# Second cross attention: the relative scores of a unit read back from DRAM as one transfer of 1 MB, behind the slot's store

## The chip, the cores and the metric

The kernel runs as one program on one core of one Trainium2 chip. The metric is the device time in microseconds (us), the median of three runs. Profile times count from the start of the profiled execution's span.

## What is computed

The reference is a small two-layer Perceiver: 256 latent tokens of width 256 attend to a context of 4096 rows, then go through self attention and a mixture of experts, twice. All of it is float32. The change lies in the cross attention of the second layer, which is a relative-position attention with 16 heads of 16 columns:

```python
content = jnp.einsum('bthd,bThd->bhtT', q + r_w_bias, k)
pe = _sinusoid_reversed(b, kv_t, DMODEL) @ Wp + bp
rel = jnp.einsum('bthd,bThd->bhtT', q + r_r_bias, pe)
rel = _relative_shift(rel)          # pad one column, read with another pitch
attn = (content + rel) * (1.0 / math.sqrt(HEAD_DIM))
attn = attn * mask - 10000000000.0 * (1.0 - mask)
p = jax.nn.softmax(attn, axis=-1)
out = jnp.einsum('bhtT,bThd->bthd', p, v)
```

The shift turns the 256 x 4096 scores of a head into rows that begin at another place: each row of 4096 scores gets a zero in front, so that rows lie 4097 apart, and the result is the same memory read with a pitch of 4096 from element 256 on.

## The kernel before, in words

`cross1` works in 64 units: 16 heads, 2 tiles of 128 queries, 2 halves of 2048 keys (16 x 2 x 2). Four units (U = 4) belong to a head. A unit of 128 x 2048 scores is handled in two parts of 128 x 1024 (SUB); here they are called its left half (part 0) and its right half (part 1).

The relative scores make a round trip through DRAM, which does the shift. For unit n + 4 TensorE computes them in slot n (`relative`, L1761), ScalarE copies both halves from PSUM into `out0` or `out1` (`evacuate`, L1886), and SP stores the unit, 1 MB, into the tensor `rel_scores` with a pitch of 4097 (`store`, L1711). Two slots later, SP reads the unit back with a pitch of 4096 into `row`, which holds eight units (`read_back`, L1698). A unit read back needs the stores of its own head that its shifted rows touch, up to the store of the unit after it.

In unit n's own slot VectorE adds the content scores from PSUM to the row (`add`, L1968), half by half; GpSimd multiplies each half with the mask (L1938, one instruction a half); VectorE takes the maximum of each half of the unit before (`top_of`, L1979); ScalarE applies the exponential to the whole unit before (`exponentials`, L1891). Three slots behind, TensorE transposes the row (`turn`, L1805), ScalarE copies the transposes (L1897), and TensorE weighs the values with them (`weigh`, L1818).

Each engine runs a hand-written list of steps per slot, with semaphores between engines. `slots` runs the filling slots -4 to 3, then a hardware loop of six passes over eight slots, then the last slots. An engine does its steps strictly in order:

- VectorE in slot n: left add of n, left maximum of n-1, right add of n, right maximum of n-1.
- ScalarE: left transposes' copy of n-3, left copy of n+4, right transposes' copy of n-3, exponential of n-1, right copy of n+4.
- TensorE: right relative scores of n+3, left content scores of n, left transposes of n-3, left relative scores of n+4, right content scores of n, right transposes of n-3, weighted sums of n-3. Content scores share one PSUM buffer, so the right ones wait for the left add.
- SP: the keys of a head to come (512 KB, once in four slots) or its values (272 KB, once in four), then left half-read of n+2, store of n+4, right half-read of n+2. The left read waits for the stores that it needs; the store waits for ScalarE's right copy.

VectorE's add of a half waits for that half's own semaphore, `rel_back[u][part]`, and for the content scores in PSUM. All transfers here are issued on SP's queue.

Of the kernel before, what the change touches and what calls it, by code (L numbers as in the profile page):

```python
# [21 lines left out]
P = 128  # L22
# [1564 lines left out]
U = NT * NHALF  # L1587
SUB = HALF // 2
CPS = SUB // P
UNITS = H * U  # L1590
ROWS_HELD = 2 * U
# [3 lines left out]
def cross1(f, mask, qw):  # L1595
# [8 lines left out]
    with ExitStack() as ctx:  # L1604
# [7 lines left out]
        with ExitStack() as inner:  # L1612
# [8 lines left out]
            rel_back = [[f.sem(f"b_rel_back{n}_{part}") for part in range(2)] for n in range(U)]  # L1621
# [65 lines left out]
            def _(sp):  # L1687
                def read_back(p, c, part, first=False):
                    n, head, u, b, t, half = where(p, c)
                    if not first:  # L1690
                        sp.wait_ge(s["turned"], 2 * n + part + 1)
                        sp.sem_inc(s["row_free"], 1)

                    for k in ((0, 1), (0, 1, 2), (2, 3), (2, 3))[u] if part == 0 else ():
                        sp.wait_ge(rel_stored[k], 16 * (head + 1))
                    columns = slice(part * SUB, (part + 1) * SUB)
                    src = rel_back_view[half][bass.ds(head, 1), t * P:(t + 1) * P, columns]
                    sp.dma_start(row[:, held(c):held(c) + 1, columns], src.rearrange("h p n -> p h n")  # L1698
                                 ).then_inc(rel_back[u][part], 16)
# [17 lines left out]
                def slot(p, c, n):  # L1717
# [11 lines left out]
                    begins = n is not None and n == -2  # L1729
                    if runs(n, 2):  # L1730
                        read_back(p, c + 2, 0, first=n is not None and n + 2 < ROWS_HELD)
                    if runs(n, 2) and begins:
                        read_back(p, c + 2, 1, first=True)
                    if runs(n, U):
                        store(p, c + U)
                    if runs(n, 2) and not begins:
                        read_back(p, c + 2, 1, first=n is not None and n + 2 < ROWS_HELD)
# [207 lines left out]
            def _(dve):  # L1945
# [16 lines left out]
                def add(p, c, part):  # L1962

                    n, head, u, b, t, half = where(p, c)
                    dve.wait_ge(rel_back[u][part], 16 * (head + 1))
                    dve.wait_ge(s["cont_mm"], 2 * n + part + 1)
                    at = part * SUB
                    nc.vector.tensor_tensor(row[:, held(c), at:at + SUB], cont_ps[:], row[:, held(c), at:at + SUB],  # L1968
                                            ALU.add).then_inc(s["cont_out"], 1)
# [772 lines left out]
```

## Time and profile before

| | |
|---|---|
| median of three runs | 1371.69 us (1367.45 to 1372.56) |
| profiled execution | 1370.89 us, its span 1369.1 us |
| mean granted TensorE clock in it | 0.929 |
| TensorE, ScalarE, VectorE, GpSimd busy | 82%, 65%, 60%, 46% of the span |
| second cross attention | about 720 to 1211 us |
| DMA traffic of the whole span | 257.53 MB, mean 188 GB/s |
| reads back in the span | 128 of 512 KB, median 6.6 us from issue to landing |
| stores of relative scores | 64 of 1 MB, median 6.1 to 6.2 us |

### The profile page before, as it was taken

To read this page: it belongs to the slowest core of one execution; us is meant where nothing else is said; L and a number is where in the kernel's file an instruction comes from. 1 tells how busy PE (TensorE), PEld (TensorE's weight loads), DVE (VectorE), ACT (ScalarE), POOL (GpSimd) and SP (SyncE) were. 2 spreads that over 40 slices of the span, in tenths; PEclk is the share of its full clock that TensorE was granted. 3 is DMA by queue.
4 is the path that set the end of the run, shared out by engine and by line. 5 is a ranking of instruction groups with operands and counts; after the bars stand their busy time and mean duration, and the time that the engine had idled before them with its cause. 6 is when DMAs were issued, how large, how long until landed. Compare 5 with 4: busy or idle time off the path is not lost. (4 is left out here: it accounts for less than half of the span.)

```text
span 1369.1 us, 25496 instructions
## 1 busy us (share of the span) xinstructions
PE 1122.3 (82%) x8423; PEld 686.5 (50%) x8423; DVE 822.0 (60%) x1502; ACT 893.6 (65%) x1204; POOL 632.2 (46%) x297
## 2 busy tenths in 40 slices
PE   7677887748999859989977878888888888858798
PEld 3343443423444346678862445455454544434687
DVE  5688888861111176562235778888888887835312
ACT  3599999967999624533323788888888888624110
POOL 2277887850000005000003889999999999900000
PEclk9899999978999968999985899999999999967899
DMA  7875455447554071024467989999999998533130
GB/s 247 256 225 134 118 130 136 116 97 158 106 113 93 0 229 45 1 70 151 152 229 255 322 292 327 327 325 332 308 324 325 327 329 311 179 114 127 47 138 8
DMA packets 97051, 257.53 MB, mean 188 GB/s; under 512 B 11193, under 2 KB 41305, under 8 KB 85466
## 3 DMA queue, kind: packets, MB, share of 16 engines
q1 hardware_dynamic: 96992, 256.79, 59.6%
q8 instruction: 32, 0.52, 0.2%
q14 instruction: 27, 0.22, 0.1%
HBM read 165.31 MB, written 91.92 MB: 188 GB/s over the span
## 5 line engine op out<-in xcount | busy, mean ns | idle before, releaser
L1938 POOL TENSOR_TENSOR xb_row<-xb_row,w_mask 128x1024 f32<-128x1024 f32 x128 | 419.1, 3286 | 237.4 <-DVE xb_row L1968 235.8
L1968 DVE TENSOR_TENSOR xb_row<-xb_cont_ps,xb_row 128x1024 f32<-128x1024 f32 x128 | 156.7, 1224 | 84.6 <-PE xb_cont_ps L1761 67.9
L1761 PE MATMUL xb_rel_ps<-xb_kk,xb_qq 32*128 32x512 f32 x496 | 150.0, 683 | 34.8 <-ACT xb_out L1886 33.2
L553 DVE TENSOR_REDUCE xa_stats<-xa_b_ps 128x1 f32<-128x1024 f32 x128 | 155.8, 1219 | 27.2 <-PE xa_b_ps L469 25.9
L1979 DVE CUSTOM_DVE_ANT_0 xb_row<-xb_row,xb_minus 128x1024 f32<-128x1024 f32 x128 | 170.4, 1331 | 0.0
L1891 ACT ACTIVATE xb_row<-xb_row,xb_ntop 128x2048 f32<-128x2048 f32 x64 | 128.3, 2005 | 53.8 <-DVE xb_ntop L1985 53.8
L1761 PE MATMUL xb_cont_ps<-xb_kk,xb_qq 32*128 32x512 f32 x528 | 160.2, 684 | 1.5 <-DVE xb_qq L2040 1.1
L868 ACT ACTIVATE xa_probs<-xa_psT,xa_t_now 128x1024 f32<-128x1024 f32 x128 | 141.2, 1114 | 24.6 <-PE xa_psT L825 24.5
L1886 ACT COPY xb_out<-xb_rel_ps 128x1024 f32<-128x1024 f32 x124 | 124.7, 1005 | 39.5 <-PE xb_rel_ps L1761 26.2
L521 ACT ACTIVATE xa_exps<-xa_b_ps,xa_stats 128x1024 f32<-128x1024 f32 x128 | 140.7, 1101 | 4.2 <-DVE xa_stats L553 4.2
L1897 ACT COPY xb_turned<-xb_turn_ps 128x1024 f32<-128x1024 f32 x126 | 127.5, 1012 | 23.2 <-PE xb_turn_ps L1805 21.1
L1805 PEld LDWEIGHTS xb_turn_ps<-_ident,xb_row 128*128 128x128 f32 x1008 | 114.7, 147 | 55.8 <-issue 55.8
L1805 PE MATMUL xb_turn_ps<-_ident,xb_row 128*128 128x128 f32 x1008 | 137.2, 280 | 5.9 <-ACT xb_turned L1897 5.1
L639 POOL TENSOR_TENSOR xa_rest<-xa_exps 128x1024 f32<-128x1024 f32 x48 | 90.9, 1894 | 90.8 <-ACT xa_exps L521 85.5
L1818 PE MATMUL xb_sum_ps<-xb_turned,xb_vhead 128*17 128x128 f32 x2048 | 81.3, 276 | 37.5 <-ACT xb_turned L1897 36.5
L1408 POOL TENSOR_TENSOR b_tc<-b_raw,w_waves 128x512 f32<-128x512 f32 x4 | 5.1, 1270 | 222.3 <-ACT b_raw L1394 222.3
L469 PE MATMUL xa_b_ps<-xa_k,xa_q 96*128 96x512 bf16 x256 | 69.8, 384 | 24.3 <-ACT xa_exps L521 13.9
L531 ACT ACTIVATE xa_squares<-xa_exps 128x1024 f32<-128x1024 f32 x80 | 84.4, 1055 | 3.0
L798 PE MATMUL xa_sums<-xa_probs,xa_vhead 128*17 128x256 f32 x1024 | 81.3, 390 | 0.2 <-ACT xa_probs L868 0.2
L490 PE MATMUL xa_b_ps<-xa_wv,xa_ctxT 128*128 x512 | 67.0, 285 | 16.0 <-ACT xa_exps L521 16.0
L1818 PEld LDWEIGHTS xb_sum_ps<-xb_turned,xb_vhead 128*17 128x17 f32 x2048 | 45.0, 97 | 66.8 <-ACT xb_turned L1897 54.7
L490 PEld LDWEIGHTS xa_b_ps<-xa_wv,xa_ctxT 128*128 128x128 f32 x512 | 61.1, 195 | 31.5 <-ACT xa_exps L521 26.4
(367 smaller groups left out, 1821.9 us busy)
## 6 DMA issues: line engine op xcount, KB each, us to landing
xb_row<-rel_scores SPq DMA_DIRECT2D x128, 512.0 KB, 6.6
rel_scores<-xb_out SPq DMA_DIRECT2D x32, 1024.5 KB, 6.2
rel_scores<-xb_out SPq DMA_DIRECT2D x32, 1024.0 KB, 6.1
b_e_w<-in_L_ffn_e_w SPq DMA_DIRECT2D x32, 513.0 KB, 3.5
w_w<-in_L_ffn_w SPq DMA_DIRECT2D x24, 512.0 KB, 4.5
xa_k<-first_parts SPq DMA_DIRECT2D x24, 384.0 KB, 4.9
value_rows<-xa_values SPq DMA_DIRECT2D x16, 544.0 KB, 6.1
xb_kk<-key_blocks SPq DMA_DIRECT2D x17, 512.0 KB, 8.2
```

The costliest lines, as they stand in the source:

```text
L490: mm = nc.tensor.matmul(out[:, n * P:(n + 1) * P], ctxT[:, k, at:at + P], wv[:, bass.ds(it, 1), k, :], start=(k == 0), stop=(k == KC - 1))
L521: nc.scalar.activation(exps[:, u % 4], ps[:, slot % 4], ACT.Exp, scale=-1.0, bias=stats[:, c % 2, 0, u:u + 1], accum_out=stats[:, c % 2, 1 ...
L553: nc.vector.tensor_reduce(stats[:, c % 2, 0, u:u + 1], ps[:, slot % 4], AX, ALU.min).then_inc(s["min_ready"], 1)
L868: nc.scalar.activation(probs[:, g % 4].rearrange("p c n -> p (c n)"), ps[:, g % 2], ACT.Exp, scale=t_now[:, b:b + 1]).then_inc(probs_ready, 1)
L1761: mm = nc.tensor.matmul(out[:, k * BANK:(k + 1) * BANK], qq[rows, b, kind, t * P:(t + 1) * P], kk[rows, b, half], start=True, stop=True)
L1805: mm = nc.tensor.transpose(out_ps[:, k * P:(k + 1) * P], row[:, held(c), at:at + P], f.ident[:])
L1818: mm = nc.tensor.matmul(sum_ps[at:at + DV, 0:P], vhead[:, b, half * NCH // 2 + part * CPS + k, :], turned[:, part, k, :], start=(part == 0 ...
L1891: nc.scalar.activation(row[:, held(c)], row[:, held(c)], ACT.Exp, bias=ntop[:, u:u + 1]).then_inc(s["exp_done"], 1)
L1897: nc.scalar.copy(turned[:, part].rearrange("p k n -> p (k n)"), turn_ps[:]).then_inc(turned_sb[part], 1)
L1938: nc.gpsimd.tensor_tensor(row[:, held(c), at:at + SUB], row[:, held(c), at:at + SUB], mask[:, t, half * HALF + at:half * HALF + at + SUB], ...
L1968: nc.vector.tensor_tensor(row[:, held(c), at:at + SUB], cont_ps[:], row[:, held(c), at:at + SUB], ALU.add).then_inc(s["cont_out"], 1)
L1979: nc.vector.tensor_tensor_reduce(out=row[:, held(c), at:at + SUB], in0=row[:, held(c), at:at + SUB], in1=minus[:, t, half * HALF + at:half ...
```

## The change

`read_back` loses its argument `part`. One transfer of 128 x 2048 float32 (1 MB, rows of 8 KB instead of 4 KB) replaces the two of 128 x 1024. It has one semaphore for each of the four units of a head, so both adds of a unit wait for the same landing. In the filling slots -2 and -1 it is issued ahead of the slot's store; in all others behind it, where until now only the right half's read stood. It waits for both transposes of the unit that held its row buffer before. The order of the steps on the other engines stays.

```diff
--- before.py
+++ after.py
@@ -1618,7 +1618,7 @@
             k_loaded, v_loaded = ([f.sem(f"{n}_loaded{b}") for b in range(2)] for n in ("k", "v"))
             turned_sb = [f.sem(f"b_turned_sb{n}") for n in range(2)]
             rel_stored = [f.sem(f"b_rel_stored{n}") for n in range(U)]
-            rel_back = [[f.sem(f"b_rel_back{n}_{part}") for part in range(2)] for n in range(U)]
+            rel_back = [f.sem(f"b_rel_back{n}") for n in range(U)]
             kk = f.sb(inner, "kk", [P, 2, NHALF, BANK])
             vhead = f.sb(inner, "vhead", [P, 2, NCH, DV])
             wq = f.sb(inner, "wq", [P, KC, D + HEAD_PAIR])
@@ -1685,18 +1685,16 @@
 
             @block.sync
             def _(sp):
-                def read_back(p, c, part, first=False):
+                def read_back(p, c, first=False):
                     n, head, u, b, t, half = where(p, c)
                     if not first:
-                        sp.wait_ge(s["turned"], 2 * n + part + 1)
+                        sp.wait_ge(s["turned"], 2 * n + 2)
                         sp.sem_inc(s["row_free"], 1)
 
-                    for k in ((0, 1), (0, 1, 2), (2, 3), (2, 3))[u] if part == 0 else ():
+                    for k in ((0, 1), (0, 1, 2), (2, 3), (2, 3))[u]:
                         sp.wait_ge(rel_stored[k], 16 * (head + 1))
-                    columns = slice(part * SUB, (part + 1) * SUB)
-                    src = rel_back_view[half][bass.ds(head, 1), t * P:(t + 1) * P, columns]
-                    sp.dma_start(row[:, held(c):held(c) + 1, columns], src.rearrange("h p n -> p h n")
-                                 ).then_inc(rel_back[u][part], 16)
+                    src = rel_back_view[half][bass.ds(head, 1), t * P:(t + 1) * P]
+                    sp.dma_start(row[:, held(c):held(c) + 1], src.rearrange("h p n -> p h n")).then_inc(rel_back[u], 16)
 
                 def store(p, c):
                     n, head, u, b, t, half = where(p, c)
@@ -1726,15 +1724,13 @@
                         if n is None or n > U:
                             sp.wait_ge(s["weighed"], 2 * U * (2 * p + c // U) + 2)
                         load_values(p, c + U)
-                    begins = n is not None and n == -2
-                    if runs(n, 2):
-                        read_back(p, c + 2, 0, first=n is not None and n + 2 < ROWS_HELD)
-                    if runs(n, 2) and begins:
-                        read_back(p, c + 2, 1, first=True)
+                    filling = n is not None and n < 0
+                    if runs(n, 2) and filling:
+                        read_back(p, c + 2, first=True)
                     if runs(n, U):
                         store(p, c + U)
-                    if runs(n, 2) and not begins:
-                        read_back(p, c + 2, 1, first=n is not None and n + 2 < ROWS_HELD)
+                    if runs(n, 2) and not filling:
+                        read_back(p, c + 2, first=n is not None and n + 2 < ROWS_HELD)
 
                 def load_values(p, c):
                     b = c // U % 2
@@ -1962,7 +1958,7 @@
                 def add(p, c, part):
 
                     n, head, u, b, t, half = where(p, c)
-                    dve.wait_ge(rel_back[u][part], 16 * (head + 1))
+                    dve.wait_ge(rel_back[u], 16 * (head + 1))
                     dve.wait_ge(s["cont_mm"], 2 * n + part + 1)
                     at = part * SUB
                     nc.vector.tensor_tensor(row[:, held(c), at:at + SUB], cont_ps[:], row[:, held(c), at:at + SUB],
```

## Rows read from the trace of the kernel before

**Rows 1.** The page's costliest groups: busy us, mean ns of one, idle before.

```profile
L1938 POOL TENSOR_TENSOR xb_row<-xb_row,w_mask 128x1024 f32<-128x1024 f32 x128 | 419.1, 3286 | 237.4 <-DVE xb_row L1968 235.8
```

**Rows 2.** SP's register moves by instruction, tile rel_scores, whole span.

```profile
L1711 SPq MOVE rel_scores<-xb_out x48: 29/29/35, 776.1 to 1112.1; - x48
```

**Rows 3.** 900:1000: length; busy PE, PEld, DVE, ACT, POOL; PEclk, DMA share, GB/s.

```profile
900.00:1000.00 100.00, 83.45 (x939) 48.93 (x938) 81.18 (x147) 83.53 (x75) 92.17 (x29) 1.00 0.92 318
```

**Rows 4.** Waits, 760 to 1180: us in total, times, longest.

```profile
POOL xb_row L1938 <- DVE xb_row L1968: 33.8, 66, 1.1
...
DVE xb_row L1968 <- DMA xb_row<-rel_scores: 15.9, 18, 1.6
```

**Rows 5.** VectorE in order of time: start us, us, instruction, idle before.

```profile
903.82 1.22 DVE L1968 TENSOR_TENSOR xb_row<-xb_cont_ps,xb_row 128x1024 f32<-128x1024 f32 x1 [0.61 <-PE xb_cont_ps L1761]
...
907.12 1.23 DVE L1968 TENSOR_TENSOR xb_row<-xb_cont_ps,xb_row 128x1024 f32<-128x1024 f32 x1 [0.85 <-PE xb_cont_ps L1761]
908.26 1.23 DVE L1979 CUSTOM_DVE_ANT_0 xb_row<-xb_row,xb_minus 128x1024 f32<-128x1024 f32 x1
...
918.08 1.23 DVE L1968 TENSOR_TENSOR xb_row<-xb_cont_ps,xb_row 128x1024 f32<-128x1024 f32 x1 [0.72 <-PE xb_cont_ps L1761]
...
921.25 1.23 DVE L1968 TENSOR_TENSOR xb_row<-xb_cont_ps,xb_row 128x1024 f32<-128x1024 f32 x1 [0.72 <-PE xb_cont_ps L1761]
```

**Rows 6.** ScalarE in order of time.

```profile
909.78 2.01 ACT L1891 ACTIVATE xb_row<-xb_row,xb_ntop 128x2048 f32<-128x2048 f32 x1 [0.61 <-DVE xb_ntop L1985]
911.69 0.99 ACT L1886 COPY xb_out<-xb_rel_ps 128x1024 f32<-128x1024 f32 x1
```

**Rows 7.** SP's queue in order of time.

```profile
906.00 0.35 SPq L1711 DMA_DIRECT2D rel_scores<-xb_out  x1
...
911.85 0.33 SPq L1698 DMA_DIRECT2D xb_row<-rel_scores  x1
912.84 0.35 SPq L1711 DMA_DIRECT2D rel_scores<-xb_out  x1
913.53 0.33 SPq L1698 DMA_DIRECT2D xb_row<-rel_scores  x1
```

**Rows 8.** Right-half reads issued at 906.70, 913.53, 920.74, 927.90: KB, us to landing.

```profile
xb_row<-rel_scores SPq DMA_DIRECT2D x1, 512.0 KB, 7.1
...
xb_row<-rel_scores SPq DMA_DIRECT2D x1, 512.0 KB, 7.5
...
xb_row<-rel_scores SPq DMA_DIRECT2D x1, 512.0 KB, 7.2
...
xb_row<-rel_scores SPq DMA_DIRECT2D x1, 512.0 KB, 6.4
```

**Rows 9.** Left-half read issued at 911.85; store issued at 722.49, nothing else in flight.

```profile
xb_row<-rel_scores SPq DMA_DIRECT2D x1, 512.0 KB, 4.9
...
rel_scores<-xb_out SPq DMA_DIRECT2D x1, 1024.5 KB, 4.2
```

**Rows 10.** TensorE in order of time.

```profile
905.90 0.70 PE L1761 MATMUL xb_cont_ps<-xb_kk,xb_qq 32*128 32x512 f32 x2
...
906.43 0.59 PE L1761 MATMUL xb_cont_ps<-xb_kk,xb_qq 32*128 32x512 f32 x2
```

**Rows 11.** Three stretches: length, PEclk, DMA share, GB/s.

```profile
724.00:726.70 2.70, 0.50 0.68 276
...
909.00:911.00 2.00, 1.00 0.95 252
1180.00:1185.00 5.00, 1.00 0.80 315
```

**Rows 12.** Content matmuls of 738 to 758, then of 900 to 1000: mean ns.

```profile
L1761 PE MATMUL xb_cont_ps<-xb_kk,xb_qq 32*128 32x512 f32 x24 | 12.5, 1136 | 0.0
...
L1761 PE MATMUL xb_cont_ps<-xb_kk,xb_qq 32*128 32x512 f32 x112 | 31.6, 639 | 0.0
```

**Rows 13.** TensorE, 1190 to 1195: length, busy, PEclk, DMA share, GB/s.

```profile
1190.00:1195.00 5.00, 3.10 (x49) 1.00 0.02 3
```

## The prediction

> **What bounds the kernel now.** I read the page's costliest groups first, then the stretches, the waits, and last single slots in order of time. The change touches only the second cross attention, some 490 us of the span; the chain of work that ended last lies in the final stage and says nothing of it. There GpSimd's mask multiplication is the largest single load: 3.29 us a half, 6.57 us a unit [rows 1]. The stores inside the hardware loop, each with one register move, show a unit's period: 48 of them from 776.1 to 1112.1 us, so 336.0/47 = 7.15 us [rows 2]. In 900 to 1000 us GpSimd is busy 92%, the DMA engines 92%, TensorE 83%, ScalarE 84% and VectorE 81% [rows 3]. Nothing is saturated, but four engines and the DMA stand close together, and GpSimd's gaps are waits for VectorE's add (33.8 us in all), while adds waited for a read from DRAM 18 times, 15.9 us together [rows 4]. So the slot is a ring of dependences, and the question is which ring a later landing closes.
>
> **The ring that the reads close.** Take the slot whose first add starts at 903.82 and call its unit m. The add of its right half starts at 907.12 [rows 5]; the right-half maximum of m-1 follows it, ScalarE's exponential starts at 909.78, the copy of the right half of m+4 at 911.69 [rows 6], and SP issues the store of m+4 at 912.84 and the right-half read of m+2 at 913.53 [rows 7]. That read takes 7.5 us [rows 8] and lands at 921.03; the right add of m+2 starts at 921.25 [rows 5]. So this ring spans two slots, and it has 0.2 us of slack: the right half arrives only just in time. The left half is another matter: issued at 911.85 [rows 7], 4.9 us long [rows 9], it lands at 916.75, and its add starts at 918.08 [rows 5], 5.24 us after the store was issued.
>
> **What the change removes and adds.** Per unit one issue of 512 KB ahead of the store goes, and the read behind the store grows from 512 KB to 1 MB. The bytes are the same. What is new is that the left add waits for the end of the whole transfer.
>
> SP's saved issue costs about 0.33 us of SP time [rows 7], and SP waits for ScalarE's copy anyway (it ends at 912.68, the store is issued at 912.84): nothing, and if that cover were gone 0.7 us a slot of earlier store at most. The wait for a free row buffer now asks for both transposes instead of one; they belong to the unit eight before, five slots back: nothing. The waits for the stores of other units move behind the store of m+4, by when they have mostly been met (the one issued at 906.00 let the left read go at 911.85): nothing. In the two filling slots before unit 0 both halves are read ahead of the store; one 0.5 MB read moves there, once: under 2 us.
>
> The term that counts is the ring. After the change the left add of m+2 waits for the landing, and from it the ring runs:
> - left add to right add. Today 907.12 - 903.82 = 3.30 us, but TensorE's content matmuls there waited for ScalarE's copy of the slot before, which with a longer slot ends in time. What remains is the add's 1.14 us (908.26 - 907.12, by the next start), some 0.1 us to TensorE, the matmuls from 905.90 to 906.43 + 0.59 = 907.02, and the 0.1 us from there to the add [rows 5, 10]: 1.14 + 0.1 + 1.12 + 0.1 = 2.46 us.
> - right add to store: 912.84 - 907.12 = 5.72 us, all of it serial (add, maximum, exponential, copy) [rows 5 to 7].
> - store to landing. The four slots of a head give 7.1, 7.5, 7.2 and 6.4 us for the right half [rows 8], and it is issued 0.70 us behind the store [rows 7]: 7.05 + 0.70 = 7.75 us on average. All four drain the same 2 MB (left half, store, right half), though the left half had up to 1.5 us of lead, or in one slot in four had mostly gone. After the change nothing of these 2 MB leads, but the queue ahead is emptier. I keep 7.75.
> - landing to add: 0.1 us.
>
> The sum is 2.46 + 5.72 + 7.75 + 0.10 = 16.03 us for two slots, 8.02 us a slot, 0.87 more than 7.15. Reads behind a store are those of units 2 to 61, 60 of them: 60 x 0.87 = 52 us. The profiled execution took 1370.9 us (span 1369.1, 1.8 around it), close to the median of 1371.7; 1370.9 + 52 = **1423 us**, 3.8% slower. GpSimd, TensorE and ScalarE get 0.9 us of idle time a slot and start nothing sooner for it; behind the waiting left add VectorE's two maxima of m-1 stand in its queue, behind the second one the exponential and the copy that lets the store go, and TensorE's right content matmul with the transposes and weighted sums behind it.
>
> **Bounds.** Store to landing is the unknown. From below: a store with nothing else in flight took 4.2 us [rows 9], and a second MB at the rate of a stretch of reads alone, 315 GB/s at a share of 0.80, so 394 at a full one [rows 11], adds 2.66: 6.9 us, 15.18 for two slots, 7.59 a slot, +26 us, 1397. From above: the longest of the four, 0.70 + 7.5 = 8.2 us, with the left-to-right step not shortened (3.30): 17.3 us for two slots, 8.66, +91 us, 1462. 7.75 lies near the rows of the same bytes in the same traffic, and those decide. The Trainium skill ("DMA: Bandwidth & Descriptors", Anatomy of one DMA) fits a transfer as 2.0 us fixed plus its bytes at 436 GB/s, fitted on another issuing path; for the 2.1 MB of store and read that is an estimate of 6.8 us and a total near 1394. The trace stands above it here: 512 KB would be 3.2 us, and 4.9 were measured in traffic [rows 9].
>
> **Rivals.**
> *The merged read makes the stage faster* (4%). For it: the DMA engines are at 0.92 and pay for changes of direction: in 909 to 911 us, where a store gives way to a read, they moved 252 GB/s at a share of 0.95 [rows 11], against 394, so some 0.7 us lost. Left, store, right has two such changes a unit, store and whole read one less. Longer packets give 276/0.68 = 406 against 394 GB/s [rows 11], 3%, 0.08 us a unit. If the DMA's load set the pace, the slot would fall until GpSimd's 6.57 and a gap of 0.2 stop it: 6.8 us, -0.35 x 60 = -21 us, 1350. It decides only if 2.1 MB land within the 5.24 us in which the left add is due. Against it: the right half, behind fewer bytes, needed 7.1 us at least. The Trainium skill ("DMA: Bandwidth & Descriptors", Bandwidth) advises transfers of at least 1 MiB for three quarters of the peak rate, which speaks for this rival; rows of transfers of 1 MB and 512 KB here differ by those 3%.
> *No change that can be measured* (6%): the ring has slack. It needs a landing within 14.30 - 2.46 - 5.72 - 0.10 = 6.0 us of the store; 1371. Only much faster draining of an emptier queue would give that.
> *TensorE's clock falls* (5%). Its busy share drops to 0.83 x 7.15/8.02 = 0.74, with a wait of over 1 us in every slot. Score matmuls average 639 ns at the full clock and 1136 at the half one [rows 12]; 0.83 x 7.15 = 5.9 us of work a slot would become 5.9 x 1136/639 = 10.5 and set the slot: with a tenth of the slots so, 6 x 2.5 = 15 us more than the forecast, 1438; with all, +200 over now, 1571. Against it: at the end of the stage a stretch with TensorE busy 62% was still granted 1.00 [rows 13]. The Trainium skill ("TensorE: Matmul & The Clock Gate", HAM oscillation) says that a wait for a transfer in each round of a loop can bring the half clock back every time.
>
> **How the numbers follow.** The ring has 85% and its own range, 1397 to 1462. Of the rest, 4% lies at 1350, 6% at 1371 and 5% above 1438. A range of 1395 to 1460 leaves out the first two (10%), the far half of the clock case (3%) and some 5% at the ring's edges. Faster by over 0.5% (6.9 us, about what a measurement of this kernel can tell from no change) 4%, within it 6%, slower 90%.
>
> **What would show it.** The period of the stores in the loop at 8.0 us (7.15); adds waiting for the read nearly 60 times, each 1 to 2 us, all on left halves; the right add about 2.5 us behind the left one; the store issued some 8.2 us after the left add (9.0); store to landing 7.75 us; GpSimd busy 82% in the stage, the DMA share about 0.82; 60 to 64 issues of 1 MB. The prediction is wrong if the merged read lands within 6 us of the store, or if the half-clock shows in the stage.

## The result, and the profile after

The changed kernel takes **1447.35 us** (median of 4, 1443.79 to 1450.38), against 1370.14 for the kernel before in the same comparison: **1.0567 times as long, interval 1.054 to 1.0595**. The forecast was 1423 us, with a range of 1395 to 1460. The direction and the range held; the forecast is 24 us too low. The profiled execution took 1447.24 us, its span 1445.4, 76.3 more than before.

The period of a slot, by SP's register moves in the loop (answers to [rows 2]), and who waited for the transfers of this tile in the whole span:

```profile
L1709 SPq MOVE rel_scores<-xb_out x48: 29/29/35, 781.7 to 1173.3; - x48
...
who waited for it (us, times):
  DVE xb_row L1964: 103.9, 55
```

(1173.3 - 781.7)/47 = 8.33 us a slot. It was 7.15; I forecast 8.02. The 47 intervals of the loop make 47 x 1.18 = 55.5 us of the 76.3. From the first store of all to the last, 63 intervals, the stores now take 72.6 us more, so 17 us come in the slots outside the loop; of the last 3.7, 3.4 lie behind the last store and 0.3 ahead of the first.

The stretch 900 to 1000 us (answers to [rows 3]: busy PE, PEld, DVE, ACT, POOL; granted clock, DMA share, GB/s), and the waits from 780 to 1240 us, in total, times, longest (answers to [rows 4]):

```profile
900.00:1000.00 100.00, 82.86 (x802) 46.67 (x804) 76.55 (x126) 70.59 (x63) 78.95 (x24) 0.95 0.76 274
```

```profile
POOL xb_row L1934 <- DVE xb_row L1964: 98.8, 57, 3.9
DVE xb_row L1964 <- DMA xb_row<-rel_scores: 90.4, 49, 3.6
ACT xb_row L1887 <- DVE xb_ntop L1981: 66.7, 52, 1.5
```

GpSimd fell from 92% to 79%, the DMA engines from 0.92 to 0.76. All engines got idle time, and the adds wait for the read 49 times instead of 18, 90.4 us instead of 15.9: a ring of waits sets the pace, no engine's load. TensorE's own share hides half-clock work, taken up below.

The ring itself, first VectorE in order of time (answers to [rows 5]; start, length, idle before):

```profile
916.47 1.22 DVE L1964 TENSOR_TENSOR xb_row<-xb_cont_ps,xb_row 128x1024 f32<-128x1024 f32 x1 [2.54 <-DMA xb_row<-rel_scores]
917.61 1.22 DVE L1975 CUSTOM_DVE_ANT_0 xb_row<-xb_row,xb_minus 128x1024 f32<-128x1024 f32 x1
...
918.92 1.23 DVE L1964 TENSOR_TENSOR xb_row<-xb_cont_ps,xb_row 128x1024 f32<-128x1024 f32 x1
920.06 2.07 DVE L1975 CUSTOM_DVE_ANT_0 xb_row<-xb_row,xb_minus 128x1024 f32<-128x1024 f32 x1
922.06 0.08 DVE L1975 DVE_READ_ACCUMULATOR2_ANT xb_top<- 128x1 f32 x1
...
924.30 1.23 DVE L1964 TENSOR_TENSOR xb_row<-xb_cont_ps,xb_row 128x1024 f32<-128x1024 f32 x1 [0.56 <-DMA xb_row<-rel_scores]
```

Then ScalarE's exponential and right copy (answers to [rows 6]), and SP's queue (answers to [rows 7]):

```profile
922.42 2.00 ACT L1887 ACTIVATE xb_row<-xb_row,xb_ntop 128x2048 f32<-128x2048 f32 x1 [1.41 <-DVE xb_ntop L1981]
924.33 0.99 ACT L1882 COPY xb_out<-xb_rel_ps 128x1024 f32<-128x1024 f32 x1
```

```profile
908.79 0.35 SPq L1709 DMA_DIRECT2D rel_scores<-xb_out  x1
909.54 0.33 SPq L1697 DMA_DIRECT2D xb_row<-rel_scores  x1
...
916.70 0.36 SPq L1709 DMA_DIRECT2D rel_scores<-xb_out  x1
917.57 0.34 SPq L1697 DMA_DIRECT2D xb_row<-rel_scores  x1
925.49 0.35 SPq L1709 DMA_DIRECT2D rel_scores<-xb_out  x1
```

And the time to landing of the store issued at 908.79 and of the read issued at 909.54, KB and us, from the DMA view (answers to [rows 8, 9]):

```profile
rel_scores<-xb_out SPq DMA_DIRECT2D x1, 1024.0 KB, 4.9
...
xb_row<-rel_scores SPq DMA_DIRECT2D x1, 1024.0 KB, 6.8
```

The read of 909.54 lands at 916.34, and the left add that needs it starts at 916.47. From there: left add to right add 918.92 - 916.47 = 2.45 us; right add to store 925.49 - 918.92 = 6.57; store to landing 916.34 - 908.79 = 7.55; landing to add 0.13. That is 16.70 us for two slots, 8.35 a slot; the loop's mean is 8.33. Left add to store is 9.02 to 9.04 us in 45 of the 48 loop slots; the other three come up below.

| term | forecast | measured |
|---|---|---|
| left add to right add | 2.46 | 2.45 |
| right add to store | 5.72 | **6.57** |
| store to landing | 7.75 | 7.55 (7.1 to 8.8 in the loop's slots, 7.45 as their mean) |
| landing to add | 0.10 | 0.13 |
| a slot | 8.02 | 8.35 |

**Where the 0.85 us come from.** The page's groups of the two instructions that stand beside each other in time, busy us and mean ns of one (the first answers to [rows 1]):

```profile
L1934 POOL TENSOR_TENSOR xb_row<-xb_row,w_mask 128x1024 f32<-128x1024 f32 x128 | 419.0, 3291 | 315.7 <-DVE xb_row L1964 315.5
...
L1975 DVE CUSTOM_DVE_ANT_0 xb_row<-xb_row,xb_minus 128x1024 f32<-128x1024 f32 x128 | 201.3, 1573 | 0.0
```

The same maxima averaged 1331 ns in the kernel before:

```profile
L1979 DVE CUSTOM_DVE_ANT_0 xb_row<-xb_row,xb_minus 128x1024 f32<-128x1024 f32 x128 | 170.4, 1331 | 0.0
```

Their work is unchanged, yet the right maximum at 920.06 is 2.07 us long where the left one is 1.22. GpSimd's row of the same moment, two mask instructions in a row:

```profile
917.77 6.58 POOL L1934 TENSOR_TENSOR xb_row<-xb_row,w_mask 128x1024 f32<-128x1024 f32 x2 [2.21 <-DVE xb_row L1964]
```

The left mask ends at 917.77 + 3.29 = 921.06, and the right maximum at about 922.13, 1.07 us behind it. The kernel before has the same distance. Its GpSimd in order of time, then its VectorE:

```profile
905.12 6.59 POOL L1938 TENSOR_TENSOR xb_row<-xb_row,w_mask 128x1024 f32<-128x1024 f32 x2 [0.26 <-DVE xb_row L1968]
...
919.38 6.59 POOL L1938 TENSOR_TENSOR xb_row<-xb_row,w_mask 128x1024 f32<-128x1024 f32 x2 [0.47 <-DVE xb_row L1968]
```

```profile
922.40 1.34 DVE L1979 CUSTOM_DVE_ANT_0 xb_row<-xb_row,xb_minus 128x1024 f32<-128x1024 f32 x1
```

Left masks end there at 908.41 and 922.67, right maxima at 908.26 + 1.23 = 909.49 [rows 5] and 922.40 + 1.34 = 923.74: 1.08 and 1.07 us later. Of the mask's typical 3283 ns its shortest record, with no maximum beside it, needs 2343; so it stretches too. By these records a maximum and a mask instruction don't run side by side: whichever starts second waits, and the wait is inside its record, not in front of it. It is so throughout: of the 44 slots 8 to 51, 42 have a right maximum longer than 1.3 us in this kernel and 22 in the kernel before, and every one of them ends 1.08 to 1.09 us after the left mask (unrounded times; 1.07 by the rounded rows above). An add (one operand in PSUM) is 1.22 to 1.23 us long beside a mask in both kernels. So the way from left add to store is left add 1.14, left maximum 1.14, the left mask's own 2.34, and 1.07 of right maximum, about 5.7 us, and then exponential and copy. The right add lies beside it. It comes 3.30 us after the left one in the kernel before and 2.45 in this one, and the store still goes 9.02 us after the left add in both (912.84 - 903.82 [rows 5, 7]; 925.49 - 916.47).

The Trainium skill ("GPSIMD Engine Reference", Specifications) has GpSimd sharing its SBUF interfaces with VectorE and contending with VectorE's instructions that have two SBUF inputs; the maximum is one (scores and mask term), the add is not. The trace agrees; the size, about 1 us for each of the two, is the runs'.

### The profile page after: what moved, and what is told of

The parts are those of the page before. It is cut to its first block and busy times, and to the rows that moved or that the text cites. A ratio compares the mean times of both kernels' runs of the same rounds, so it can differ in the third digit from the quotient of the medians.

```text
span 1445.4 us, 25230 instructions
## 1 busy us (share of the span) xinstructions
PE 1180.1 (82%) x8423; PEld 709.4 (49%) x8423; DVE 852.8 (59%) x1502; ACT 893.0 (62%) x1204; POOL 632.2 (44%) x297
## 5 line engine op out<-in xcount | busy, mean ns | idle before, releaser
L1975 DVE CUSTOM_DVE_ANT_0 xb_row<-xb_row,xb_minus 128x1024 f32<-128x1024 f32 x128 | 201.3, 1573 | 0.0
L1757 PE MATMUL xb_cont_ps<-xb_kk,xb_qq 32*128 32x512 f32 x528 | 166.2, 708 | 11.3 <-DVE xb_row L1964 9.8
L1893 ACT COPY xb_turned<-xb_turn_ps 128x1024 f32<-128x1024 f32 x126 | 127.5, 1012 | 73.1 <-PE xb_turn_ps L1801 72.6
L1801 PEld LDWEIGHTS xb_turn_ps<-_ident,xb_row 128*128 128x128 f32 x1008 | 121.4, 153 | 55.3 <-issue 55.3
L1801 PE MATMUL xb_turn_ps<-_ident,xb_row 128*128 128x128 f32 x1008 | 146.4, 292 | 2.2 <-ACT xb_turned L1893 1.8
L1814 PE MATMUL xb_sum_ps<-xb_turned,xb_vhead 128*17 128x128 f32 x2048 | 89.9, 299 | 33.0 <-ACT xb_turned L1893 30.9
L1814 PEld LDWEIGHTS xb_sum_ps<-xb_turned,xb_vhead 128*17 128x17 f32 x2048 | 48.2, 103 | 67.8 <-ACT xb_turned L1893 52.2
L1757 PEld LDWEIGHTS xb_rel_ps<-xb_kk,xb_qq 32*128 32x128 f32 x496 | 40.2, 198 | 81.2 <-ACT xb_out L1882 64.6
```

Source lines behind the costliest of these rows:

```text
L1757: mm = nc.tensor.matmul(out[:, k * BANK:(k + 1) * BANK], qq[rows, b, kind, t * P:(t + 1) * P], kk[rows, b, half], start=True, stop=True)
L1801: mm = nc.tensor.transpose(out_ps[:, k * P:(k + 1) * P], row[:, held(c), at:at + P], f.ident[:])
L1814: mm = nc.tensor.matmul(sum_ps[at:at + DV, 0:P], vhead[:, b, half * NCH // 2 + part * CPS + k, :], turned[:, part, k, :], start=(part == 0 ...
L1893: nc.scalar.copy(turned[:, part].rearrange("p k n -> p (k n)"), turn_ps[:]).then_inc(turned_sb[part], 1)
L1975: nc.vector.tensor_tensor_reduce(out=row[:, held(c), at:at + SUB], in0=row[:, held(c), at:at + SUB], in1=minus[:, t, half * HALF + at:half ...
```

## The experiments

The comparisons are with the kernel before on the same chip (medians 1369.5 to 1371.5). A period is that of SP's register moves in the loop, as above. Line numbers differ from kernel to kernel.

**The place of the read.** Three kernels separate where the read stands from how large it is. The first keeps the one transfer of 1 MB but issues it ahead of the store in every slot.

```diff
-                    filling = n is not None and n < 0
-                    if runs(n, 2) and filling:
-                        read_back(p, c + 2, first=True)
+                    if runs(n, 2):
+                        read_back(p, c + 2, first=n is not None and n + 2 < ROWS_HELD)
                     if runs(n, U):
                         store(p, c + U)
-                    if runs(n, 2) and not filling:
-                        read_back(p, c + 2, first=n is not None and n + 2 < ROWS_HELD)
```

> The changed kernel with the 1 MB read issued ahead of the slot's store everywhere instead of behind it. Theory (position: what costs is that the left half's landing moved behind the store, and a ring of two slots closes through it): the read goes when the store of the slot before lands, the ring becomes one of three slots, 9.0 us from left add to store, some 6.5 from store to landing, some 6 for the read, so 21.6/3 = 7.2 us a slot, near the kernel before: 1370 to 1390 us. Rival (size: a transfer of 1 MB as such comes too late wherever it stands): a slot of 8.3 us as in the changed kernel, about 1447.

Measured: 1427.69 us, ratio 1.0415 (1.0366 to 1.0465), period 8.04. Neither theory gave this. One turn, on VectorE, then SP's queue, then the landing of the store of 902.20 and of the read of 910.81:

```profile
891.51 1.22 DVE L1961 TENSOR_TENSOR xb_row<-xb_cont_ps,xb_row 128x1024 f32<-128x1024 f32 x1 [0.28 <-PE xb_cont_ps L1754]
...
917.38 1.23 DVE L1961 TENSOR_TENSOR xb_row<-xb_cont_ps,xb_row 128x1024 f32<-128x1024 f32 x1 [1.97 <-DMA xb_row<-rel_scores]
```

```profile
901.58 0.33 SPq L1697 DMA_DIRECT2D xb_row<-rel_scores  x1
902.20 0.35 SPq L1709 DMA_DIRECT2D rel_scores<-xb_out  x1
...
910.81 0.34 SPq L1697 DMA_DIRECT2D xb_row<-rel_scores  x1
```

```profile
rel_scores<-xb_out SPq DMA_DIRECT2D x1, 1024.0 KB, 8.4
...
xb_row<-rel_scores SPq DMA_DIRECT2D x1, 1024.0 KB, 6.4
```

The store behind 1 MB of read lands after 8.4 us, not 4.9, and the next read that needs its rows is issued 0.2 us after it has landed (902.20 + 8.4 = 910.6). So another ring closes, over three slots. This turn of it is 917.38 - 891.51 = 25.9 us: left add to store 10.7, store 8.4, 0.2, read 6.4, and the rest to the add; 8.6 us a slot. The mean period is less, because the read of a head's fourth unit needs no store of the slot before it and goes early. Left add to store is no longer fixed: it goes from 9.0 to 12.6 us in the loop, once to 14.0, since ScalarE waits 31 times, 60.0 us in the span, for the landing of a store that gives back an out buffer (the adds wait 70.3 us, 33 times, for a read). Which of the two waits is worth how much stays open. The merged read is slower than the kernel before in either place.

The second keeps two halves, and issues both behind the store (the filling slots as in the changed kernel).

```diff
-                    if runs(n, 2):
-                        read_back(p, c + 2, 0, first=n is not None and n + 2 < ROWS_HELD)
...
                     if runs(n, U):
                         store(p, c + U)
-                    if runs(n, 2) and not begins:
-                        read_back(p, c + 2, 1, first=n is not None and n + 2 < ROWS_HELD)
+                    if runs(n, 2) and not filling:
+                        for part in range(2):
+                            read_back(p, c + 2, part, first=n is not None and n + 2 < ROWS_HELD)
```

> Only the position of the change, not its size: two reads of 512 KB, both behind the store, each add with its own semaphore. Theory (each add waits for its own bytes, so part of the loss is the merging and part the position): the left half lands some 1.3 to 1.5 us before the whole did, 6.0 us after the store instead of 7.4, and the ring gives (9.0 + 6.0 + 0.1)/2 = 7.55 us a slot, about 1400 us. Rival (position alone costs all): 8.3 us a slot, about 1447. Rival (merging alone costs all): 7.15 us, about 1371.

Measured: 1427.56 us, 1.0423 (1.0365 to 1.0481), period 8.02. It lies between the theory's 1400 and the rival's 1447: the left half lands 6.9 us after the store, not 6.0. VectorE in order of time, for the left half issued at 910.71 behind the store of 909.85:

```profile
900.81 1.22 DVE L1968 TENSOR_TENSOR xb_row<-xb_cont_ps,xb_row 128x1024 f32<-128x1024 f32 x1 [1.68 <-DMA xb_row<-rel_scores]
...
916.87 1.23 DVE L1968 TENSOR_TENSOR xb_row<-xb_cont_ps,xb_row 128x1024 f32<-128x1024 f32 x1 [0.74 <-DMA xb_row<-rel_scores]
```

The half's time to landing is 6.0 us, so it lands at 916.71, 6.9 us after the store. Ring: left add to store 909.85 - 900.81 = 9.04, and (9.04 + 6.86 + 0.16)/2 = 8.03. So, taken in this order, **about 57 of the 77 us are the left half's place behind the store, and 20 are the joining of the halves** (the two ratios' intervals lie apart). The split holds behind the store only. The joining costs 0.31 us a slot, 0.62 in the ring of two slots, where half a MB at the 394 GB/s of [rows 11] would be 1.3. The right half, issued at 911.38, lands at 917.98, 8.1 us after the store, so the whole transfer lands between the two halves: joined, it is later for the left add and sooner for the right one.

The third issues both half reads ahead of the store.

```diff
-                    begins = n is not None and n == -2
                     if runs(n, 2):
-                        read_back(p, c + 2, 0, first=n is not None and n + 2 < ROWS_HELD)
-                    if runs(n, 2) and begins:
-                        read_back(p, c + 2, 1, first=True)
+                        for part in range(2):
+                            read_back(p, c + 2, part, first=n is not None and n + 2 < ROWS_HELD)
                     if runs(n, U):
                         store(p, c + U)
-                    if runs(n, 2) and not begins:
-                        read_back(p, c + 2, 1, first=n is not None and n + 2 < ROWS_HELD)
```

> Two reads of 512 KB, both ahead of the store. Theory (ring of three slots: 9.0 us from left add to store, 8.4 us for a store behind 1 MB of reads, 0.2 us, some 5 us until the left half lands, 0.1 us): 22.7/3 = 7.6 us a slot, about 1398. Rival (only the store's own place counts, as with the whole read ahead): 8.05 us, 1427.

Measured: 1437.94 us, 1.0511 (1.0484 to 1.0538), mean period 8.04. Neither expectation gave this: it is later than the whole read ahead. Its stores land after 7.0 to 10.7 us in the loop, and ScalarE now waits 68.8 us (28 times) for a store to give back an out buffer, twice the adds' 31.5. The waits name the late store; no run takes it away alone. Here the single transfer was the better one, by 10 us (1427.69 against 1437.94). The traces show little of that: the loops have the same period, and the two profiled executions lie 4.5 us apart (1426.47 and 1430.98). Why is open.

**What sets the 9.0 us from left add to store.** In the changed kernel, GpSimd masks only the first 512 of the 1024 columns of each half; the other 512 are left out.

```diff
-                        nc.gpsimd.tensor_tensor(row[:, held(c), at:at + SUB], row[:, held(c), at:at + SUB],
-                                                mask[:, t, half * HALF + at:half * HALF + at + SUB],
+                        nc.gpsimd.tensor_tensor(row[:, held(c), at:at + SUB // 2], row[:, held(c), at:at + SUB // 2],
+                                                mask[:, t, half * HALF + at:half * HALF + at + SUB // 2],
                                                 ALU.mult).then_inc(s["masked"], 1)
```

> The changed kernel with GpSimd's mask multiplication on the first 512 of the 1024 columns of each half (the multiplication of the other 512 is left out). Theory (the right maximum cannot run beside GpSimd's instruction and waits for the left mask, so left add, left maximum, left mask, right maximum set the 9.0 us from left add to store): the left mask is over some 1.2 us earlier, the right add's path of 8.2 us takes over, and the slot falls from 8.3 to 7.9 us, about -25 us, 1422; the right maximum's record falls from 2.07 to near 1.2 us. Rival (as the prediction had it: the path is right add, maximum, exponential, copy, and GpSimd has idle time): no change, 1447, and the long record stays.

Measured: 1418.86 us, 1.035 (1.0304 to 1.0396), period 7.98, as the theory had it. VectorE in order of time:

```profile
900.80 1.22 DVE L1964 TENSOR_TENSOR xb_row<-xb_cont_ps,xb_row 128x1024 f32<-128x1024 f32 x1 [1.79 <-DMA xb_row<-rel_scores]
...
903.25 1.22 DVE L1964 TENSOR_TENSOR xb_row<-xb_cont_ps,xb_row 128x1024 f32<-128x1024 f32 x1
904.39 1.22 DVE L1975 CUSTOM_DVE_ANT_0 xb_row<-xb_row,xb_minus 128x1024 f32<-128x1024 f32 x1
```

```profile
908.98 0.36 SPq L1709 DMA_DIRECT2D rel_scores<-xb_out  x1
```

The right maximum is back at 1.22 us, the store (the row of SP's queue) goes 908.98 - 900.80 = 8.18 us after the left add, and the store goes 5.73 us after the right add: with the mask out of the way, the 5.72 of the prediction comes back. GpSimd was busy 79% in the changed kernel and idle 2.2 us ahead of each pair, and still its instruction stood on the path.

The same edit in the kernel before, to see whether the mask paces that one:

> The kernel before with GpSimd's mask multiplication on the first 512 of the 1024 columns of each half (the other 512 are left out). Theory (in the kernel before the left half's landing is not late, so the left mask sets only the copy and the store, and the right read's ring of 14.1 us is nearly as long as two slots of 14.3): the slot falls to 7.05 us at most, 0 to -6 us, 1366 to 1372. Rival (the kernel before is paced by GpSimd and VectorE taking turns): the slot falls by about 0.5 us or more, 1340 or less.

Measured: 1364.08 us, 0.9954 (0.9926 to 0.9982), period 7.10. The same edit is worth 28 us where the ring runs through the mask, and 6 where it hardly does.

**TensorE's clock.** The stretch above was granted 0.95 on average. Pieces of it (length, TensorE busy, granted clock, DMA share, GB/s):

```profile
900.00:902.00 2.00, 2.00 (x5) 0.52 1.15 393
902.00:904.00 2.00, 2.00 (x12) 0.50 0.88 279
904.00:906.00 2.00, 1.89 (x36) 0.50 0.95 389
```

So the clock did drop to 1.2 GHz in some slots, and the two stores around this stretch lie 9.93 us apart (898.86 and 908.79). VectorE's adds of that turn:

```profile
898.70 1.22 DVE L1964 TENSOR_TENSOR xb_row<-xb_cont_ps,xb_row 128x1024 f32<-128x1024 f32 x1 [2.61 <-DMA xb_row<-rel_scores]
...
902.02 1.23 DVE L1964 TENSOR_TENSOR xb_row<-xb_cont_ps,xb_row 128x1024 f32<-128x1024 f32 x1 [0.86 <-PE xb_cont_ps L1757]
```

The right add waited for TensorE, 3.32 us after the left one, and left add to store took 908.79 - 898.70 = 10.09 us instead of 9.03. Does this cost anything in the mean? I added matmuls (128 x 128, into a part of PSUM that nothing reads) in every slot of the changed kernel, first three ahead of the left relative scores and three ahead of the right content scores:

```diff
+                def keep_busy():
+                    for k in range(EXTRA):
+                        nc.tensor.matmul(sum_ps[:, 2 * P:3 * P], f.ident[:], f.ident[:], start=True, stop=True)
...
+                    spare = n is None or BEHIND < n < UNITS
+                    if spare:
+                        keep_busy()
                     if runs(n, U):
...
+                    if spare:
+                        keep_busy()
                     if runs(n, 0):
```

> The changed kernel with six more matmuls of 128x128 a slot into an unused part of a PSUM bank, three ahead of the left relative scores and three ahead of the right content scores, where TensorE waits. Theory (the clock fell to one half in some slots because TensorE waits, and each such slot is 1.5 to 2 us longer): the granted clock of the stage goes from 0.95 to 0.98 to 1.00, slots of over 9 us vanish in the loop, -10 to -15 us, 1435. Rival (the half-clock slots cost nothing, the ring of the read sets the slot anyway): 1447. Rival (the extra 0.8 us ahead of each score matmul lands in the ring): slower by 10 to 50 us.

Measured: 1486.29 us, 1.0845 (1.0796 to 1.0894), period 9.09; the clock 1.00, TensorE 93% busy, and the adds wait for TensorE. The extra work landed on the path, between the left add and the right one, as the second rival had it, and the run says nothing on the clock. It does say something on the mask. Where the right add comes this late (5.06 us after the left add of 899.21), its maximum no longer meets the left mask, which runs from 900.51 to 903.77, and is 1.22 us long with the mask whole:

```profile
904.27 1.23 DVE L1974 TENSOR_TENSOR xb_row<-xb_cont_ps,xb_row 128x1024 f32<-128x1024 f32 x1 [2.61 <-PE xb_cont_ps L1758]
905.41 1.22 DVE L1985 CUSTOM_DVE_ANT_0 xb_row<-xb_row,xb_minus 128x1024 f32<-128x1024 f32 x1
```

No right maximum in its slots 8 to 51 is longer than 1.3 us. The second try has only the first three matmuls:

> As the run before with extra matmuls, but only the three ahead of the left relative scores, where TensorE waits 1.1 us in each slot for ScalarE's copy; the three ahead of the right content scores are gone. Theory (slots at half clock cost time, and the loss of the first try was the extra work standing in the path of the right scores): granted clock 1.00 in the loop, no slot over 9 us, 10 to 20 us less than the changed kernel, 1430 to 1437. Rival (half-clock slots are free because the read's ring sets the pace): 1447. Rival (0.8 us of extra work does not fit even there): above 1447.

```profile
900.00:1000.00 100.00, 86.22 (x875) 52.31 (x874) 76.39 (x126) 70.71 (x64) 78.60 (x24) 1.00 0.76 275
```

Measured: 1447.93 us, 1.0564 (1.052 to 1.0609), period 8.40. The stretch 900 to 1000 now has the full clock throughout and the time is the same, but this is no clean test, as the same row for most of the loop shows, first of the changed kernel, then of this one:

```profile
782.00:1173.00 391.00, 317.63 (x3146) 178.53 (x3140) 299.71 (x494) 277.89 (x246) 308.55 (x94) 0.97 0.76 276
```

```profile
782.00:1173.00 391.00, 338.15 (x3413) 206.96 (x3411) 295.40 (x489) 275.58 (x245) 305.90 (x94) 0.98 0.75 273
```

The half clock came in other slots and hardly less often (0.98 against 0.97), and the three matmuls may cost time of their own. What the half clock costs is better read from the changed kernel's own ring. Of its six half-clock stretches in the loop, two met the path: left add to store took 10.08 us (unrounded, the turn above) and 10.04 us, and in the same two places the other slots' ring waited for TensorE, with a left add 1.05 us behind its landing instead of 0.13. That makes some 2 us in each of the two interleaved rings, so about 2 us of the 1447, an estimate from these rows; the other four stretches cost at most half a us. (The third slot off the 9.03 us, with 9.46, had the full clock.)

**Can the landing be pulled ahead?** A store in two halves of 512 KB, the left one issued as soon as ScalarE has copied the left half. In the changed kernel, the 1 MB read behind the right one:

```diff
-                def store(p, c):
+                def store(p, c, part):
                     n, head, u, b, t, half = where(p, c)
-                    sp.wait_ge(s["rel_out"], 2 * n + 3)
+                    sp.wait_ge(s["rel_out"], 2 * n + 2 + part)
...
                     if runs(n, U):
-                        store(p, c + U)
+                        for part in range(2):
+                            store(p, c + U, part)
                     if runs(n, 2) and not filling:
```

> The changed kernel with the store in two halves, the left one issued as soon as ScalarE has copied it; the 1 MB read stays behind the right one. Theory (ring of left add, store, landing): from the right store's issue 1.5 MB are queued instead of 2, the whole read lands 6.1 to 6.3 us after it instead of 7.4, and (9.0 + 6.2 + 0.1)/2 = 7.65 us a slot, 1405 to 1410. Rival (the landing is bound by the read itself, not by the store ahead of it): 8.3 us a slot, 1447.

Measured: 1451.43 us, 1.0575 (1.053 to 1.062), period (1183.2 - 782.8)/47 = 8.52. This is the rival's time. The read still lands 6.8 to 9.5 us after the right half of the store in the loop, 7.8 as a mean, though only 512 KB are issued there; it takes 6.0 to 8.8 us of its own. The left store of the next slot is issued 1.3 to 2.5 us behind the read and shares the engines with it, so the bytes moved until the landing are the same 2 MB or so. Fewer bytes ahead of the read did not bring its landing forward; whether the read's own time or the traffic beside it sets the landing, this run doesn't separate.

In the kernel before, the halves of the store stand around the left read (in the filling slots both reads stand ahead of both):

> The kernel before with the store in two halves as well: left half stored as soon as ScalarE has copied it, then the left read, the right store, the right read. Theory (the time from store to landing closes the rings, and it is the bytes queued behind ScalarE's last copy that count): 1 MB instead of 1.5 to 2 MB is queued then, the right read lands some 6.2 us after the right store instead of 7.75, the right read's ring falls to about 12.6 us, and whatever else paces the slot comes out: 6.8 to 7.0 us a slot, 1350 to 1362. Rival (the right read's ring did not pace the kernel before, or rows of 4 KB make the engines slower): 1371 or more.

Measured: 1368.48 us, 0.9977 (0.9959 to 0.9994), not the theory's 1350 to 1362. The right half lands 6.6 us after the last store of its slot instead of 7.7 (means of the loop), the adds wait for a read 3.6 us in all, twice, and the time moves by 0.2%. So the reads' ring, which I had found with 0.2 us of slack, was not what paced the kernel before; it was only close.

**The order of the adds.** TensorE computes the right content scores ahead of the left relative ones, so that the right add can follow the left one sooner.

```diff
                         turn(p, c - BEHIND, 0)
+                    if runs(n, 0):
+                        content(p, c, 1)
                     if runs(n, U):
...
-                    if runs(n, 0):
-                        content(p, c, 1)
                     if runs(n, -BEHIND):
```

In the kernel before:

> The kernel before with one change of order on TensorE: the right content scores of a slot are made ahead of the left relative scores instead of behind them. Theory (what paced the kernel before was a ring of one slot, exponential, right copy, left relative scores with the right content scores behind them, right add, right maximum, exponential, 7.1 to 7.2 us): the right content scores no longer wait for ScalarE's copy, the right add starts 2.5 us behind the left one instead of 3.3, and the slot falls to what GpSimd's 6.6 us and the read's rings (13.6 to 14.1 us for two slots) leave: 6.85 to 7.05 us, 1353 to 1365. Rival (the left relative scores come later and ScalarE's left copy with them, or the read's ring holds the slot): 1368 to 1373, or slower.

Measured: 1367.67 us, 0.9994 (0.9978 to 1.001), period 7.10. VectorE in order of time:

```profile
899.75 1.22 DVE L1968 TENSOR_TENSOR xb_row<-xb_cont_ps,xb_row 128x1024 f32<-128x1024 f32 x1 [0.39 <-PE xb_cont_ps L1761]
...
902.20 1.22 DVE L1968 TENSOR_TENSOR xb_row<-xb_cont_ps,xb_row 128x1024 f32<-128x1024 f32 x1
903.34 2.06 DVE L1979 CUSTOM_DVE_ANT_0 xb_row<-xb_row,xb_minus 128x1024 f32<-128x1024 f32 x1
```

The right add comes 2.45 us after the left one here, as in the changed kernel (2.85 us as a mean of the loop), and the right maximum behind it takes 2.06 us, as in the changed kernel. Left add to store keeps its median of 9.03 us. The expected gain did not come. This is the failed step of the prediction by itself, with no change to any transfer: what the right add gains, the maximum spends waiting for the mask.

In the changed kernel:

> The same change of order in the changed kernel. Theory (there the ring through the read paces the slot: left add, mask, right maximum, exponential, copy, store 9.0 us, landing 7.4 us; the right add is not in it): no change, 8.3 us, 1443 to 1450. Rival (the right add is in the ring, as the prediction had it): some 0.1 to 0.4 us a slot less, 1420 to 1440.

Measured: 1452.44 us, 1.0621 (1.0569 to 1.0672), period 8.40. No gain, as expected: its interval overlaps that of the changed kernel. Left add to store keeps its median of 9.03 us.

Both edits together, halved stores and right content first, in the kernel before:

> The kernel before with the right content scores first and the store in two halves, the left one ahead of the left read. Theory (the one-slot ring is cut by the order, and what is left are the read's rings, which the earlier half store shortens): 6.8 to 6.95 us a slot, 1350 to 1358, at or under the run with the order alone. Rival (the order alone already leaves GpSimd's 6.6 us plus its gap as the bound, or 4 KB rows and one more issue a slot take back the gain): the same as with the order alone.

Measured: 1365.27 us, 0.9971 (0.9959 to 0.9983), 4 us under the kernel before, where the theory had 1350 to 1358. It is the fastest version that leaves nothing out, but by less than the 0.5% that tells a change here.

## Why the prediction was right, and where it was not

- **The mechanism held.** The left add waits for the merged read, the ring runs over two slots through add, maximum, exponential, copy, store and landing, and the measured parts sum to the measured period. In the halves behind the store a ring of the same form, with its own measured landing, sums to their period too (8.03 for 8.02); ahead of the run I had taken that landing 0.9 us too early.
- **The step that failed** is "right add to store: 912.84 - 907.12 = 5.72 us, all of it serial". It was read from a slot in which the right add came late enough to meet a mask that was about to end. I shortened the step ahead of it by 0.84 us and left it alone; but the right maximum waits for the left mask, which starts at the left add. Left add to store stays at 9.02 us and does not fall to 8.18. The slot was also one of the quick ones: right add to store is 5.72 in it and 5.95 as a mean of the loop of before. In the changed kernel the step measures 6.57: +0.85. The trace of before showed it: right maxima of 1.23 and 1.34 us in [rows 5] and beside it, ending 1.07 after each left mask, and a mask record of 3.29 us against a shortest one of 2.34.
- **Store to landing** was taken at 7.75 and measures 7.45 as a mean: right in size. That "all four drain the same 2 MB" was right for the number. It is not shown as the reason: with the store in halves fewer bytes stood ahead of the read, and its landing was no sooner.
- **The sum mended:** (0.85 - 0.01 + 0.03 - 0.20)/2 = 0.33 us a slot, 60 x 0.33 = 20 of the 24 us. The other 4 are too small to split: the growth holds over 63 intervals, not 60, and 3.7 us lie outside the stores.
- **The bound from above** was right in part by luck: it left the left-to-right step at 3.30, for another reason, and with 5.72 that is the 9.02 that was measured.
- **Rivals.** *Faster* and *no change* needed a landing within 5.24 or 6.0 us of the store; the shortest in the loop was 7.1. The 3% better rate of longer packets is beside the point when the DMA engines stand at 0.76. The Trainium skill ("DMA: Bandwidth & Descriptors", Bandwidth) advises transfers of at least 1 MiB, for their rate. Behind the store no run here shows a gain from it: joining the halves cost 20 us. Ahead of the store the joined read was 10 us better than the halves, for a reason that is open. *TensorE's clock* did fall in some slots, to a mean of 0.97 over the loop; by the ring's rows that is worth some 2 us, so this rival's condition came true, and not its price. The prediction named the half clock in the stage as a sign that it is wrong; the sign showed, and was too strict.
- **What would show it.** Period 8.33 for 8.0; 49 to 55 waits for nearly 60, on left halves; right add 2.45 us behind the left, as said; store 9.0 us behind the left add instead of 8.2, which is the miss; GpSimd 79% for 82%, which is what the longer slot makes of it; the DMA share 0.76 for 0.82, where the longer slot alone would give 0.79; 64 reads of 1 MB. SP's saved issue, the changed waits and the filling slots cost nothing that shows in any wait.

What paces the kernel before at 7.15 us stays open. Relieving the reads' ring, the right add or (in part) the mask each moves the time by 0.5% or less, the first two together by 0.3%: several rings of nearly one length seem to stand there, but no run separates them.

## What to carry to other kernels

Joining two transfers makes the first byte's user wait for the last byte: ask first which of the halves stood ahead of what, and run the ring through the landing. Where a step of a ring is shortened, look at every instruction behind it for one that waits on another engine from an earlier point, since the gain ends there. A record that is longer than its shortest twin can hold a wait, as the right maximum's does here, though no view of waits lists it. And a sum of terms is only as good as the turn that they come from: check them against one whole turn and the mean period.

## What the runs showed of the hardware

- A VectorE maximum with two SBUF operands and a GpSimd multiplication, each of 128 x 1024, exclude each other: 2.07 instead of 1.22 us for a maximum that starts second, 3.28 instead of 2.34 us for a mask that does. VectorE's adds with one operand in PSUM are not touched (1.22 to 1.23 us).
- A store of 1 MB lands after 4.9 us when it is issued ahead of a read of 1 MB, and after 8.4 us behind it; the read needs 6.8 us behind the store and 6.4 ahead of it. In these two kernels, coming second cost the store 3.5 us and coming first gave the read 0.4.
- Behind a store, the first of two reads of 512 KB lands some 0.6 us sooner than one read of 1 MB, and the second some 0.6 us later (6.9 and 8.1 against 7.45 to 7.55 us after the store).
- Stretches of TensorE at half its clock cost little where rings through other engines are in charge: of six in the loop, two met the path, and each made one turn some 1.0 us longer (10.08 and 10.04 instead of 9.03 us from left add to store).
